# Audio tower on one core: patch tile 1 loaded ahead of the token weights, the token bias as one fp32 row that opens each accumulator, all norm roots on ScalarE

## What is computed

```
x = layer_norm(x, g1, b1, 1e-6)                 # 448 x 1024
x = einsum('bpd,dh->bph', x, W) + b             # 1024 -> 512, the token bias b
h = layer_norm(x, g2, b2, 1e-6)
h = h + attention(layernorm(h, 1e-5))           # 16 heads of 128, causal over the 7 patches
h = h + ffn(layernorm(h, 1e-5))                 # x rounded to fp8, W 512 x 512, bias
```

## Time and profile before

| | us |
|---|---|
| median of 3 runs | 269.01 (268.57 to 269.03) |
| the profiled execution | 268.16 |
| its span | 266.4 |
| busy PE / DVE / ACT | 256.4 / 159.5 / 124.8 |
| mean granted TensorE clock | 0.991 |

### The profile page before, as it was taken

One profiled execution on the slowest core, in us unless ns is written; L12 is line 12 of the kernel. 1 busy time (PEld: TensorE's weight loads), 2 busy tenths in 40 slices (PEclk: granted clock), 3 DMA queues, 4 the chain that ended last, 5 costly groups with the idle time before them and its releaser, 6 DMA issues.

```text
span 266.4 us, 3864 instructions
## 1 busy us (share of the span) xinstructions
PE 256.4 (96%) x1434; PEld 219.8 (83%) x1434; DVE 159.5 (60%) x325; ACT 124.8 (47%) x215; POOL 0.2 (0%) x4
## 2 busy tenths in 40 slices
PE   7799999899899999999999999999999999999994
PEld 6344446898799999999999999999999999998672
DVE  5268996833926903872394269138722967934884
ACT  2666964354534542534362435325443642546680
POOL 0000000000000000000000000000000000000000
PEclk9999999999999999999999999999999999999888
DMA  6999030033071053023305210530240020000004
GB/s 180 332 277 387 11 119 0 2 123 113 0 253 65 2 197 118 1 60 137 118 0 171 64 80 0 197 118 0 43 153 0 2 79 0 2 0 0 0 4 138
DMA packets 7627, 23.63 MB, mean 89 GB/s; under 512 B 1261, under 2 KB 1725, under 8 KB 7488
## 3 DMA queue, kind: packets, MB, share of 16 engines
q1 hardware_dynamic: 7616, 23.48, 26.9%
HBM read 22.56 MB, written 0.92 MB: 88 GB/s over the span
## 4 chain that ended last, share of the span: by engine, by line
PE 88%; DMA 4%; DVE 3%; SPq 2%; issue 1%; ACT 1%; DVEq 0%; ACTq 0%
PE bank L315 14%; PE bank L317 14%; PE bank L316 14%; PE acc L459 9%; PE acc L350 9%; PE bank L434 5%; PE bank L443 5%; PE acc L463 4%; DMA tokw_raw<-tok_w 4%; PE acc L653 3%; PE bank L449 3%; PE bank L426 2%; SPq L248 2%; PE bank L523 2%; PE bank L639 1%; PE bank L339 1%
## 5 line engine op out<-in xcount | busy, mean ns | idle before, releaser
L315 PE MATMUL bank<-ht_hi,qkvw_hi 128*128 128x448 f32 (+1 forms) x192 | 69.4, 362 | 0.9 <-issue 0.9
L317 PE MATMUL bank<-ht_hi,qkvw_lo 128*128 128x448 f32 (+1 forms) x192 | 69.1, 360 | 0.0
L316 PE MATMUL bank<-ht_lo,qkvw_hi 128*128 128x448 f32 (+1 forms) x192 | 69.0, 359 | 0.0
L948 DVE TENSOR_TENSOR qkvw_lo<-raw_qkv,qkvw_hi 128x1536 fp32r<-128x1536 f32 x16 | 28.1, 1754 | 35.6 <-ACT qkvw_hi L685 35.6
L315 PEld LDWEIGHTS bank<-ht_hi,qkvw_hi 128*128 128x128 f32 x192 | 36.1, 188 | 3.9 <-issue 1.3
L317 PEld LDWEIGHTS bank<-ht_hi,qkvw_lo 128*128 128x128 f32 x192 | 36.1, 188 | 2.7
L316 PEld LDWEIGHTS bank<-ht_lo,qkvw_hi 128*128 128x128 f32 x192 | 36.1, 188 | 2.6
L350 PE MATMUL acc<-tokw_raw,xt 128*112 128x512 f32 x64 | 29.7, 600 | 1.7 <-DMA tokw_raw<-tok_w 1.3
L685 ACT CAST qkvw_hi<-raw_qkv 128x1536 fp32r<-128x1536 f32 x16 | 23.5, 1477 | 0.0
L350 PEld LDWEIGHTS acc<-tokw_raw,xt 128*112 128x112 f32 x64 | 10.4, 176 | 15.4 <-issue 9.6
L1154 DVE COPY prob_t<-bank 112x448 f32<-112x448 f32 x8 | 5.0, 625 | 29.0 <-PE bank L426 29.0
(11 more groups left out here) (148 smaller groups left out, 396.5 us busy)
## 6 DMA issues: line engine op xcount, KB each, us to landing
raw_qkv<-heads_w SPq DMA_DIRECT2D x16, 768.0 KB, 4.3
raw_out<-heads_w SPq DMA_DIRECT2D x16, 256.0 KB, 4.5
tokw_raw<-tok_w SPq DMA_DIRECT2D x4, 512.0 KB, 7.4
x_in<-patches SPq DMA_DIRECT2D x3, 448.0 KB, 11.2
ffnw_raw<-ffn_w SPq DMA_DIRECT2D x1, 1024.0 KB, 16.4
out<-h_sb SPq DMA_DIRECT2D x3, 224.0 KB, 2.6
x_in<-patches SPq DMA_DIRECT2D x2, 224.0 KB, 3.0
g_row<-tok_g SPq DMA_DIRECT2D x1, 224.0 KB, 10.7
```

The source lines that it names most:

```text
L315: nc.tensor.matmul(ps, hi, whi, start=first, stop=False, skip_group_check=True)
L316: nc.tensor.matmul(ps, hi, wlo, start=False, stop=False, skip_group_check=True)
L317: return nc.tensor.matmul(ps, lo, whi, start=False, stop=last, skip_group_check=True)
L948: return nc.vector.tensor_tensor(dst, src, hi.bitcast(F32), ALU.subtract)
```

## The change

- Loads: the bias is one row of 512 (`tok_b_row`), issued third; patch tile 1 goes ahead of all token weight pieces. The other loads keep their order.
- Bias: `begin_with_bias` multiplies a row of ones with the bias row in fp32 and opens `acc[t]`; for tiles 1 to 3 right after the warm-up, for tile 0 behind its transposes. L357, the split, its two conversions and two semaphores are gone. The last product of a tile now closes the accumulator.
- Warm-up: 5 products in place of 14.
- TensorE: the transposes of patch tile 1 stand behind the sixth product of tile 0; those of the others stay after the fourth product of the tile before.
- Roots: all twelve norms are in `ROOTS`; the Newton branch is gone. One multiplication in the Newton step is a scalar_tensor_tensor in place of a tensor_scalar with two pointers.
- ScalarE's order: see the diff.

```diff
-WARM_START, WARM_STATS, WARM_RSTD, WARM_SCALE = 14, 2, 3, 3
+WARM_START, WARM_STATS, WARM_RSTD, WARM_SCALE = 5, 2, 3, 3
...
+            load(tok_b_row[:], tok_b[0:1, :], tok_b_landed)
             load(ident_sb[:], ident, ident_landed)
             load(g1_col[:], tok_g1, cols_landed)
             load(b1_col[:], tok_b1, cols_landed)
+            load(x_in[:, 1, :], patches[1], x_landed[1])
             load_tokw(0)
-            load(tok_b_raw[:], tok_b, tok_b_landed)
             load_tokw(1)
-            load(x_in[:, 1, :], patches[1], x_landed[1])
             load_tokw(2)
             load_tokw(3)
...
+            def begin_with_bias(t):
+                nc.tensor.matmul(acc[t][0:TR, :], ones_sb[0:1, :], tok_b_row[:], start=True, stop=False,
+                                 skip_group_check=True)
...
             pe.wait_ge(ones_ok, 2)
             keep_warm(WARM_START, acc[TILES - 1])
+            pe.wait_ge(tok_b_landed, 16)
+            for t in range(1, TILES):
+                begin_with_bias(t)
             patch_transposes(0)
...
+            begin_with_bias(0)
+            embed(0, {KIN - 2: lambda: patch_transposes(1)})
+            embed(1, {KIN // 2: lambda: patch_transposes(2)})
+            embed(2, {KIN // 2: lambda: patch_transposes(3)})
+            stream_transposes(0)
+            embed(3, {KIN // 2: lambda: stream_transposes(1)})
             stream_transposes(2)
...
-            act.wait_ge(tok_b_landed, 16)
-            hi_part(tok_b_split[:], tok_b_raw[:]).then_inc(tok_b_hi_ok, 1)
             take_root(1)
             normalise(1)
-            patch_evacuate(1, between=lambda: take_root(2))
+            patch_evacuate(1)
+            take_root(2)
             normalise(2)
             take_root(3)
             take_root(TILES)
+            patch_evacuate(2)
             normalise(3)
-            patch_evacuate(2)
+            take_root(2 * TILES)
+            take_root(TILES + 1)
             split_qkv(0, 0)
+            normalise_stream(0)
+            patch_evacuate(3, between=lambda: take_root(2 * TILES + 1))
+            normalise_stream(1)
+            stream_evacuate(0)
+            take_root(TILES + 2)
             split_qkv(0, 1)
             split_out(0, 0)
-            normalise_stream(0)
-            take_root(2 * TILES + 1)
-            patch_evacuate(3)
-            stream_evacuate(0)
-            take_root(TILES + 2)
-            normalise_stream(1)
+            take_root(2 * TILES + 2)
             stream_evacuate(1)
-            take_root(2 * TILES + 2)
             normalise_stream(2)
...
-                    done[c] = mark(nc.vector.tensor_scalar(n, y, y, v, ALU.mult, ALU.mult))
+                    done[c] = mark(nc.vector.scalar_tensor_tensor(out=n, in0=y, scalar=v, in1=y,
+                                                                  op0=ALU.mult, op1=ALU.mult))
...
-            need(rsqrt([(1, LN_EPS)], patch_moments(1)))
-            negative_mean_scaled(1).then_inc(x_scaled, 1)
...
+            for t in (1, 2):
+                patch_moments(t)
+                need(rsqrt_from_roots([t]))
+                negative_mean_scaled(t).then_inc(x_scaled, 1)
+            patch_moments(3)
             dve.wait_ge(rows_landed, 32)
-            stream_norms(0, None, patch=(3, patch_moments(3)))
+            stream_norms(0, None, patch=3)
```

More of the change, by code:

```diff
@@ L12 @@
 BF16 = mybir.dt.bfloat16
-I32 = mybir.dt.int32
 BATCH, PATCHES = 64, 7
@@ L38 @@
 LN_EPS, NORM_EPS = 1e-6, 1e-5
-ROOTS = {0: LN_EPS, 1: LN_EPS, 2: LN_EPS, 3: LN_EPS, TILES: LN_EPS, 2 * TILES + 1: NORM_EPS, TILES + 2: LN_EPS,
-         2 * TILES + 2: NORM_EPS, TILES + 3: LN_EPS, 2 * TILES + 3: NORM_EPS}
+ROOTS = {0: LN_EPS, 1: LN_EPS, 2: LN_EPS, 3: LN_EPS, TILES: LN_EPS, 2 * TILES: NORM_EPS, TILES + 1: LN_EPS,
+         2 * TILES + 1: NORM_EPS, TILES + 2: LN_EPS, 2 * TILES + 2: NORM_EPS, TILES + 3: LN_EPS,
+         2 * TILES + 3: NORM_EPS}
+NORM_ROOT = list(ROOTS).index(2 * TILES)
 FP8_MAX, SCALE_EPS = 448.0, 1e-7
@@ L342, in patch_transposes, with embed @@
                         mm.then_inc(xt_ps, 1)
-            def embed(t, half, within=None):
-                for k in range(half * KIN // 2, (half + 1) * KIN // 2):
+            def begin_with_bias(t):
+                nc.tensor.matmul(acc[t][0:TR, :], ones_sb[0:1, :], tok_b_row[:], start=True, stop=False,
+                                 skip_group_check=True)
+            def embed(t, ahead_of):
+                for k in range(KIN):
+                    if k in ahead_of:
+                        ahead_of[k]()
                     for i, (first_chunk, _) in enumerate(TOKW_PIECES):
@@ L349, in embed @@
                     pe.wait_ge(xt_ok, KIN * t + k + 1)
[L350 to L358, removed]
+                    last = nc.tensor.matmul(acc[t][0:TR, :], xt[:, t % 2, k * TR:(k + 1) * TR], tokw_raw[:, k, :],
+                                            start=False, stop=(k == KIN - 1), skip_group_check=True)
+                last.then_inc(tok_ps, 1)
             def stream_transposes(t):
@@ L877, in take_last_roots @@
                 nc.scalar.activation(last_root[:], moments[:, LAST:LAST + TILES, 1], ACT.Sqrt,
-                                     bias=eps_4[:, 1:2], scale=4.0).then_inc(last_root_ok, 1)
+                                     bias=eps_4[:, NORM_ROOT:NORM_ROOT + 1], scale=4.0).then_inc(last_root_ok, 1)
             def scale_rows(t):
@@ L956, in moments_of, with need_moments @@
                 link(last)
[L957 to L966, removed]
+                nc.vector.bn_aggr(moments[:, c, :], stats[:, c, 0:len(parts), :]).then_inc(variance_ok, 1)
+            def need_moments(c):
+                dve.wait_ge(variance_ok, list(ROOTS).index(c) + 1)
             def rsqrt_from_roots(columns, between=None):
@@ L990, in rsqrt_from_roots @@
                                                                   op0=ALU.add, op1=ALU.mult))
[L991 to L1017, removed]
                 return max(done.values())
@@ L1027, in patch_moments @@
                 dve.wait_ge(x_landed[t], 16)
-                return moments_of(t, [x_in[:, t, i * 512:(i + 1) * 512] for i in range(IN_DIM // 512)],
-                                  x0_rest_landed if t == 0 else None)
+                moments_of(t, [x_in[:, t, i * 512:(i + 1) * 512] for i in range(IN_DIM // 512)],
+                           x0_rest_landed if t == 0 else None)
             def stream_lo(t):
@@ L1039, in stream_lo @@
                         ht_hi[:, :, c]).then_inc(ht_lo_ok, 1)
-            stream_step = {}
             def stream_norms(t, own, between=None, patch=None):
-                columns, step = [], 0
+                columns = []
                 if t is not None:
@@ L1050, in stream_norms @@
                     dve.wait_ge(tok_ps, t + 1)
-                    step = moments_of(c, [acc[t][0:TR, :]])
-                    need_moments(c, step)
+                    moments_of(c, [acc[t][0:TR, :]])
+                    need_moments(c)
                     centred_step = mark(nc.vector.scalar_tensor_tensor(
@@ L1056, in stream_norms @@
                         op0=ALU.subtract, op1=ALU.mult))
-                    columns.append((c, LN_EPS))
+                    columns.append(c)
                 if patch is not None:
-                    step = max(s for s in (step, patch[1], 0) if s is not None)
-                    columns.append((patch[0], LN_EPS))
+                    columns.append(patch)
                 if own is not None:
-                    step = max(s for s in (step, stream_step[own], 0) if s is not None)
-                    columns.append((2 * TILES + own, NORM_EPS))
-                need(rsqrt(columns, step, between))
+                    columns.append(2 * TILES + own)
+                need(rsqrt_from_roots(columns, between))
                 if patch is not None:
-                    negative_mean_scaled(patch[0]).then_inc(x_scaled, 1)
+                    negative_mean_scaled(patch).then_inc(x_scaled, 1)
                 if own is not None and own < TILES - 1:
@@ L1097, in _ @@
                 nc.vector.memset(eps_4[:, i:i + 1], 4.0 * eps).then_inc(eps_ok, 1)
-            need(rsqrt([(0, LN_EPS)], patch_moments(0)))
+            patch_moments(0)
+            need(rsqrt_from_roots([0]))
             negative_mean_scaled(0).then_inc(x_scaled, 1)
```

31 lines of the change are left out of this document (3 added, 28 removed).

## The result

| | before | after |
|---|---|---|
| median, us | 268.28 (267.08 to 269.03, 6 runs) | 271.13 (270.51 to 272.22, 6 runs) |
| ratio | | 1.0114 (95%: 1.0079 to 1.0149) |
| profiled execution / its span | 268.16 / 266.4 | 272.22 / 270.4 |

The change makes the kernel 1.1% slower. 266.5 was forecast, with a range up to 267.9. It is the rival (c) that came true. The forecast stood on the first three executions of the kernel before (269.01); against that base it said 0.9% faster. A ratio is formed from executions taken on one chip and is not exactly the quotient of the two medians.

What follows compares the result with a forecast made beforehand. It took the attention loop's matmuls as the bound, untouched, and the front (TensorE, then VectorE's last norm) as what changes. Gains 1.71 + 0.6 + 0.22 = 2.5 us from the 269.01 median gave 266.5, range 265.7 to 267.9.

Steps and rivals of the forecast that it cites:

- rival (c): Slower: TensorE still at 1.2 GHz when tile 0's products begin; tile 0 ends at 22.2, total 270.5 us; chance 0.07.
- the part on the start: Warm-up and bias rows before tile 0: 0.4 us late, ends 0 and 2.4; lateness up to 1.2 costs nothing.
- Bias, tiles 1 to 3: TensorE from tile 0's end to the last accumulator: 24.67 us becomes 22.96 without closing bias products; gain 1.71.
- Tile 0: Third weight piece lands at 13.7 (13.2 to 14.1), so the first tile ends at 18.2, not 18.79; gain 0.6 us.
- Patch tile 1 covered: Its norm ends near 13.2 us, TensorE wants it at 15.7: ready with 2.5 us to spare.
- Roots worth nothing by themselves: Tile 1's norm without the Newton chain: 1.1 us less on VectorE, no gain by itself, useful as cover.
- Tail: VectorE's norm of the last tile: two cheaper Newton multiplies, 159 for 272 ns each; gain 0.22 us (0 to 0.25).
- ScalarE's order: Evacuations, roots and splits moved on ScalarE: nothing on the path, three places within 0.5 us.
- The sum: Gains of 1.71, 0.6 and 0.22 make 2.5 us: span 263.9, profiled time 265.7, median 266.5.

Runs made afterwards that it cites:

- run 1: The change with all 14 warm-up products in place of 5: 271.58 us, ratio 1.0108 to the kernel before.
- run 2: The change with 9 warm-up products, meant to leave no hole before the bias rows: 269.46 us, ratio 1.0056 to the kernel before.
- run 10: Kernel before plus four unused products on zeros behind the 14 warm-ups: over one row 273.72 us, ratio 1.0239; over 112 rows 269.29 us, ratio 1.0059.
- run 3: The change with bias products over all 112 rows, 111 of them zeros, still 5 warm-up products: 266.20 us, ratio 0.9946 to the kernel before.
- run 8: The change with full-row bias products, 6 warm-ups, bias row issued by ScalarE's queue: 264.88 us, ratio 0.9889 to the kernel before; repeated 264.58, ratio 0.9878.
- run 9: As run 8, but weight pieces 0 and 1 ahead of patch tile 1, its transposes after the seventh product: 265.33 us, ratio 0.9907 to the kernel before.
- run 6: Kernel before with only all twelve roots on ScalarE and the new Newton multiply: 267.02 us, ratio 1.0002 to the kernel before.
- run 7: The change with bias products over all 112 rows and 7 warm-up products: 265.30 us, ratio 0.9923 to the kernel before.

## Why the prediction was wrong

**The step that failed** is in the part on the start: "I take 0.4, since the engine's work before 5.4 is nearly what it was; the ends are 0 and 2.4 of lateness, a loss of 0 to 1.2." I counted the bias rows as TensorE work like any other. The runs show otherwise. With one-row products the clock stayed low until 18 us (the change) or fell (runs 1, 2 and 10), and with 112 rows in the same instructions it rose and stayed (run 3) or did not fall (run 10). The lateness was the upper end, 2.4 (9.6 for 7.2), and that end was priced wrongly too: its loss of 1.2 held only for products at 2.4 GHz, and the first ones ran at half speed: six of tile 0's sixteen halves, after the bias rows and the transposes. By the trace the low clock lasted until 18, through bias rows, transposes and the first products.

**Rival (c)** named this mechanism with 0.07 and priced it at 270.5 with two slow products (three were); the median is 271.13. The nearness of these totals is partly luck of the base. Rival (c) is 1.5 us over the 269.01 that it started from, and the change is 2.9 over 268.28. Its chain has tile 0 end at 22.2 against 23.5: 0.9 for the third slow product, 0.4 for transposes and fourth bias row (1.68 and 1.98 us in place of 1.54 and 1.72). Its point of decision, "the first product is still at the low clock", was the right one. Its arguments were unequal: for it stood holes between the weight pieces, of which there were none; the one-row products were named in half a sentence. The row I leaned on against it, no fall over the 1.26 us hole, was about idling and could not speak about busy one-row work. The trace of before has no product over fewer than the 33 rows of L357, so this was a cost to be bounded from both sides, with the whole of tile 0 at half speed as the upper end, inside the range.

The rule weighed against the change (the Trainium skill, TensorE: Matmul & The Clock Gate, What's actually happening: throttled by default, released by sustained activity) agrees with the trace if one-row products are taken as no activity; runs 3 and 10 show that they must be here.

**Bias, tiles 1 to 3**: right. 24.67 became 22.9 in the change and in the versions without the closing product (40.13 less 17.2 in run 8's repetition); forecast 22.96. (Run 9, with its wait for tile 2, has 23.7.)

**Tile 0**: the arithmetic is right where the clock is up, the landing was wrong. The third piece landed at 11.6, not 13.7 (range 13.2 to 14.1), the last at 13.3 against 15.59. The 66 KB bias load with its 33 rows is gone and the order is another, but executions of one queue differ too (12.8 and 13.5), so how much belongs to the change stays open. It is a benefit that the change could not use: the products were the bound.

**Patch tile 1 covered**: right; normalised by 15.75 (forecast 13.2) with the root queued behind the evacuations, though tile 0's evacuation began 2.8 us later than before (10.66), and wanted at 21.

**Roots worth nothing by themselves**: right as far as run 6 can tell. That they serve as cover wasn't tried by itself. **Tail**: forecast 0.22, found 0.10 (5.59 for 5.69). The new multiply takes

```profile
51.04 0.22 DVE L969 SCALAR_TENSOR_TENSOR newton<-rstd,vscaled 112x1 f32<-112x1 f32 x1
```

not 159 ns, as its neighbours with an immediate scalar do: the pointer costs in this form too, 0.22 against 0.27.

**ScalarE's order**: right that nothing there was on the path in the change; run 9 shows how near it is.

**The sum**: the front part without the clock would have been 2.5 us under the kernel before by my numbers. Run 7, which keeps all of the change and only repairs the clock, has 0.9923, which is 2.1 us. That the two agree is partly luck. By the chains TensorE gets the last norm at 45.62 in run 7, 3.6 us sooner than in the profiled execution of before, since tile 0 ends at 17.1 with the early pieces and not at 18.2. But that execution took 268.16 where the medians of before on the chips of the runs are 267.25 to 267.81, and run 6, with the same queue, has the norm at 48.21. Against run 6 the gain is 2.6; the last 0.5 are open. One trace of before was too little to set the landing by.

## What to carry to other kernels

A busy TensorE was not enough here to keep its clock up: at the same clock a product over one row takes as long as one over 112 (587 and 592 ns an instruction), but the clock stayed low or fell with it. Where filling or opening products stand at the start or between waits, give them all rows (zeros did in runs 3 and 10), and judge the clock by the durations of equal instructions, not by the granted clock alone. And when an added instruction has no row in the trace, the range must hold both of its ends, including what it does to the work behind it.

## What was not expected of the hardware

- One-row fp32 products of 512 columns, gapless for 5.5 us, left the clock at 1.2 GHz; 4.7 us of them brought it down from 2.4 (granted 0.82, then 0.71), while the same with 112 rows kept 1.00 (one profiled execution of each).
- At the same clock one row and 112 rows take the same: 587 and 592 ns an instruction, 0.43 us from start to start.
- The low clock of the start is not in the granted clock (1.00 from 4 to 18 us in the change); a fall after a rise is (0.57 from 10 to 18 us in run 1).
- The time of the rise differs between executions of one kernel: bias rows of 4.29 and 3.63 us in two profiles of run 8.
